# Four 32-column variance tiles a chunk, 128x128 roots between the sigmoids, centring 16 chunks ahead

## The reference, cut to what matters

```
xn    = (x - mean) * rsqrt(var + 1e-5)          # over the 64 channels
left  = (xn @ Wl) * mask * sigmoid(xn @ Wlg)    # layer 3: no mask
right = (xn @ Wr) * mask * sigmoid(xn @ Wrg)
gate  = sigmoid(xn @ Wog)
out   = einsum('bikd,bjkd->bijd', left, right)
out   = layernorm(out) * gate @ Wout
```

## Time and profile before

| | us |
|---|---|
| median of 3 runs (2088.78 to 2090.52) | 2089.22 |
| the profiled execution | 2091.39 |
| its span, which the rows count from | 2089.3 |
| PE busy | 1770.6 (85%) |
| ACT busy | 1372.3 (66%) |
| DVE busy | 1319.1 (63%) |
| POOL busy | 1031.0 (49%) |

### The profile page before, as it was taken

The page is one execution under the profiler, slowest core; times in us unless marked ns, Lnnn a source line. Parts: engine busy times, 40 slices in busy tenths (PEclk is TensorE's granted clock), DMA queues, the critical chain, the costliest instruction groups (busy, mean ns, idle before and its releaser), DMA issues. The chain is left out here.

```text
span 2089.3 us, 41026 instructions
## 1 busy us (share of the span) xinstructions
PE 1770.6 (85%) x10389; PEld 1045.5 (50%) x10389; DVE 1319.1 (63%) x2920; ACT 1372.3 (66%) x2541; POOL 1031.0 (49%) x1044
## 2 busy tenths in 40 slices
PE   0889997797998899985699799799799998699776
PEld 0444454685554444444355477643344444588533
DVE  7566666124763677775977388466377778344675
ACT  0577876365996777774599566477478787244554
POOL 0267678003991677786899200089122223000599
PEclk9999998898999999998899899999899999899999
DMA  7357876774996265647499666189557776845599
GB/s 327 124 184 236 245 232 216 271 297 169 365 367 235 97 189 168 193 135 264 146 357 366 231 226 207 35 321 385 175 157 227 237 236 216 296 174 228 193 398 373
DMA packets 326947, 496.15 MB, mean 237 GB/s; under 512 B 22828, under 2 KB 188463, under 8 KB 320439
## 3 DMA queue, kind: packets, MB, share of 16 engines
q1 hardware_dynamic: 326838, 494.93, 68.4%
HBM read 285.12 MB, written 197.13 MB: 231 GB/s over the span
## 5 line engine op out<-in xcount | busy, mean ns | idle before, releaser
L809 POOL TENSOR_TENSOR lo<-xn,hi 128x512 f16<-128x512 f32 x192 | 224.1, 1167 | 373.5 <-DVE hi L736 231.9
L601 PE MATMUL ps<-w_heads,hi 64*128 64x256 f16 x3072 | 292.8, 273 | 11.7 <-POOL lo L809 4.7
L1118 ACT ACTIVATE O<-ps 128x512 f32 (+1 forms) x144 | 151.7, 1054 | 189.3 <-PE ps L1042 189.3
L750 DVE SCALAR_TENSOR_TENSOR sig<-ps,largest,sig 128x512 f32<-128x512 f32 x256 | 180.7, 746 | 145.4 <-ACT sig L664 144.5
L664 ACT ACTIVATE sig<-ps,largest 128x512 f32<-128x512 f32 x384 | 246.1, 692 | 32.2 <-PE ps L601 23.3
L1355 POOL TENSOR_TENSOR shared<-O,out_rs 128x128 f32<-128x128 f32 (+1 forms) x112 | 76.3, 683 | 371.0 <-DVE out_rs L1255 370.0
L645 ACT ACTIVATE zs<-ps,shift 128x512 f32<-128x512 f32 x192 | 132.0, 687 | 192.9 <-PE ps L569 188.9
L601 PEld LDWEIGHTS ps<-w_heads,hi 64*128 64x128 f16 x3072 | 153.2, 95 | 169.3 <-DVE sig L750 67.0
L1403 PEld LDWEIGHTS ps<-ident,shared 128*128 128x128 f32 (+1 forms) x1024 | 120.2, 133 | 224.8 <-issue 96.8
L1403 PE MATMUL ps<-ident,shared 128*128 128x128 f32 (+1 forms) x1024 | 160.8, 282 | 76.6 <-POOL shared L1355 49.2
L601 PE MATMUL ps<-w_heads,lo 64*128 64x256 f16 x1536 | 212.8, 272 | 0.0
(11 more groups left out here) (168 smaller groups left out, 3787.6 us busy)
## 6 DMA issues: line engine op xcount, KB each, us to landing
shared<-left_right SPq DMA_DIRECT2D x34, 2048.0 KB, 12.0
shared<-gate SPq DMA_DIRECT2D x224, 256.0 KB, 4.6
gate<-gates SPq DMA_DIRECT2D x96, 512.0 KB, 2.9
x_dram<-shared SPq DMA_DIRECT2D x192, 256.0 KB, 4.3
shared<-x_dram SPq DMA_DIRECT2D x192, 256.0 KB, 4.7
xs<-x_dram SPq DMA_DIRECT2D x64, 512.0 KB, 4.2
left_right<-stage SPq DMA_DIRECT2D x64, 448.0 KB, 5.9
left_right<-shared SPq DMA_DIRECT2D x64, 448.0 KB, 5.9
```

What stands on the lines that cost most here:

```text
L601: last = pe.matmul(PAIR[row][:, g, kb * S:kb * S + S], tokens[half, q % 8, at:at + P], k["w_heads"][half, part, :], start=(step == 0), sto ...
L750: dve.scalar_tensor_tensor(dst, pair(row, 1), k["largest"][:, 1:2], factor, ALU.mult, ALU.mult).then_inc(pair_read.sem, 1)
L809: pool.tensor_tensor(lo[:, q % 8, :], xn[:, q % 2, :], hi[:, q % 8, :], ALU.subtract).then_inc(c["lo_done"].sem, 1)
L1118: act.activation(o_of(ch), ps[h % 4 // 2][:, h % 2, :].rearrange("p (b g i) -> p b g i", b=2, g=2), ACT.Copy).then_inc(c["o_copied"].sem, 1)
```

## The change

- VAR becomes 128x128: the 512 positions are cut in four, and each quarter has its own 32 columns of the array and its own 32 partitions of the bank. Variance is four f32 matmuls (8 instructions) of 128 positions each, in place of one (2 instructions) of 512.
- Ln, Exp and the split work on 128x128 in place of 16x512. The split writes `terms`; SP then moves its rows to `r_terms` with 12 DMAs of 16x128 a batch (4 for the first term, 8 for the two others a step later), and spread waits for them.
- Leads: CENTER 16, VARIANCE 15, LOAD 20. Variance stands ahead of the heads in PE's step.
- The rings of `hi` and `lo` go from 8 to 4, and SP's loop is written out.

```diff
-    LOAD, CENTER, VARIANCE, SPLIT, NORM = 14, 12, 11, 3, 2
+    LOAD, CENTER, VARIANCE, SPLIT, MOVE, NORM = 20, 16, 15, (7, 6), (6, 5), 2
+    R_PARTS, MOVES = 2, 3 * CH // P
...
-        Z, VAR, R, GATE = ps[0][:, 0, :], ps[0][:, 1, :], ps[1][:, 0, :], ps[1][:, 1, :]
+        Z, VAR, R, GATE = ps[0][:, 0, :], ps[0][:, 1, 0:P], ps[1][:, 0, :], ps[1][:, 1, :]
...
+            def move_high(i, b):
+                batch = i * (BODY // BATCH) + b
+                sp.wait_ge(c["r_high"].sem, c["r_high"](batch + 1))
+                sp.wait_ge(c["spread_done"].sem, c["spread_done"](batch * BATCH - BATCH))
+                move(0, b)
+            def move_low(i, b):
+                sp.wait_ge(c["r_split"].sem, c["r_split"](i * (BODY // BATCH) + b + 1))
+                move(1, b)
+                move(2, b)
+            def move(term, b):
+                for quad in range(CH // P):
+                    sp.dma_start(r_terms[R_PART * term:R_PART * term + 2 * BATCH, b % 2, quad * P:quad * P + P],
+                                 terms[quad * QUAD:quad * QUAD + 2 * BATCH, term, :]).then_inc(c[f"r_moved{b % 2}"].sem, 16)
             def step(i, q, more, first=False):
+                for part, lead in zip((move_high, move_low), MOVE):
+                    if more(lead) and (q + lead) % BATCH == 0:
+                        part(i, (q + lead) // BATCH)
                 if q % 2 == 0 and more(LOAD):
                     load(i, q + LOAD)
...
-                w = k["var_w"][:, 2 * (BATCH - 1 - at):2 * (BATCH - 1 - at) + P]
-                pe.matmul(VAR, w, sq[:, q % 2, :], start=(at == 0), stop=(at == BATCH - 1)).then_inc(c["var_done"].sem, 1)
+                first = 2 * (BATCH - 1 - at)
+                for quad in range(CH // P):
+                    last = pe.matmul(VAR[quad * QUAD:quad * QUAD + QUAD, :], k["var_w"][:, first:first + QUAD],
+                                     sq[:, q % 2, quad * P:quad * P + P], start=(at == 0), stop=(at == BATCH - 1))
+                last.then_inc(c["var_done"].sem, 1)
...
             def spread(i, q):
-                pe.wait_ge(c["r_split"].sem, c["r_split"](i * (BODY // BATCH) + b + 1))
+                moved = c[f"r_moved{b % 2}"]
+                pe.wait_ge(moved.sem, moved((i * (BODY // BATCH // 2) + b // 2 + 1) * MOVES * 16))
...
                 if more(CENTER):
                     center(i, q + CENTER, Z, i * BODY + q + CENTER)
+                if more(VARIANCE):
+                    variance(i, q + VARIANCE)
                 heads(i, q, 0)
                 heads(i, q, 1)
                 out_gate(i, q)
-                if more(VARIANCE):
-                    variance(i, q + VARIANCE)
...
-                act.activation(log_var[:], VAR[0:2 * BATCH, :], ACT.Ln, bias=k["unit"][0:2 * BATCH, 2:3]).then_inc(c["log_done"].sem, 1)
+                act.activation(log_var[:], VAR, ACT.Ln, bias=k["unit"][:, 2:3]).then_inc(c["log_done"].sem, 1)
...
-                dve.tensor_copy(terms[0], r[:]).then_inc(parts.sem, 1)
...
-                dve.tensor_tensor(terms[2], r_rest[:], r_mid[:], ALU.subtract).then_inc(split.sem, 1)
+                dve.tensor_copy(terms[:, 0, :], r[:]).then_inc(c["r_high"].sem, 1)
...
+                dve.tensor_tensor(r_rest[:], r[:], terms[:, 0, :], ALU.subtract).then_inc(parts.sem, 1)
...
+            def split_low(i, b):
...
+                dve.tensor_copy(terms[:, 1, :], r_rest[:]).then_inc(parts.sem, 1)
...
+                dve.tensor_tensor(terms[:, 2, :], r_rest[:], terms[:, 1, :], ALU.subtract).then_inc(c["r_split"].sem, 1)
```

More of the change, by code:

```diff
@@ L459, in project @@
         xs, zs, sq = sb("xs", [P, 8, CH]), sb("zs", [P, 16, CH]), sb("sq", [P, 2, CH])
[L460 to L461 removed]
+        log_var, r, r_rest = sb("log_var", [P, P]), sb("r", [P, P]), sb("r_rest", [P, P])
+        terms = sb("terms", [P, 3, P], BF16)
         r_terms = sb("r_terms", [P, 2, CH], BF16)
[L463 removed]
+        xn, hi, lo = sb("xn", [P, 2, CH]), sb("hi", [P, 4, CH], F16), sb("lo", [P, 4, CH], F16)
         sig, gates = sb("sig", [P, 4, CH]), sb("gates", [P, 4, CH])
@@ L543, in _ @@
                 load(0, q)
+            move_high(0, 0)
+            move_low(0, 0)
             for q in range(BODY):
                 step(0, q, lambda lead: True, first=True)
-            with sp.Fori(1, bodies - 1) as i:
+            for i in range(1, bodies):
                 for q in range(BODY):
-                    step(i, q, lambda lead: True)
-            for q in range(BODY):
-                step(bodies - 1, q, lambda lead: q + lead < BODY)
+                    step(i, q, lambda lead: i * BODY + q + lead < NCH)
             sp.wait_ge(c["lr_done"].sem, c["lr_done"](NCH * 2))
@@ L600, in heads @@
                             half = slice(g * C, g * C + C)
-                            last = pe.matmul(PAIR[row][:, g, kb * S:kb * S + S], tokens[half, q % 8, at:at + P],
+                            last = pe.matmul(PAIR[row][:, g, kb * S:kb * S + S], tokens[half, q % 4, at:at + P],
                                              k["w_heads"][half, part, :], start=(step == 0), stop=(step == 2))
@@ L665, in gate_pair @@
                                ACT.Sigmoid, scale=k["largest"][:, 0:1]).then_inc(c["sig_done"].sem, 1)
-            def root_step(i, q, more):
-                if more(VARIANCE) and (q + VARIANCE) % BATCH == BATCH - 1:
-                    root(i, (q + VARIANCE) // BATCH)
             def step(i, q, more):
@@ L676, in step @@
                 gate_pair(i, q, 1)
-                root_step(i, q, more)
+                if more(VARIANCE) and (q + VARIANCE) % BATCH == BATCH - 1:
+                    root(i, (q + VARIANCE) // BATCH)
                 act.wait_ge(c["gate_mm_done"].sem, c["gate_mm_done"](m + 1))
@@ L688, in _ @@
                     root(0, 0)
-            start = (2 * BATCH - 1 - VARIANCE) % BATCH + 1
-            for q in range(start):
-                step(0, q, lambda lead: True)
+            step(0, 0, lambda lead: True)
             with act.Fori(0, bodies - 2) as i:
-                for q in range(start, start + BODY):
+                for q in range(1, 1 + BODY):
                     step(i, q, lambda lead: True)
-            for q in range(start, 2 * BODY):
+            for q in range(1, 2 * BODY):
                 step(bodies - 2, q, lambda lead: q + lead < 2 * BODY)
@@ L755, in step @@
                     norm(i, q + NORM)
-                if more(SPLIT) and (q + SPLIT) % BATCH == 0:
-                    split_r(i, (q + SPLIT) // BATCH)
+                for split, lead in zip((split_high, split_low), SPLIT):
+                    if more(lead) and (q + lead) % BATCH == 0:
+                        split(i, (q + lead) // BATCH)
                 left_and_right(i, q)
@@ L831, in project @@
     batches = NCH // BATCH
-    for name in ("log_done", "r_done", "r_split"):
+    for name in ("log_done", "r_done", "r_high", "r_split"):
         c[name].advance(batches)
-    c["r_part"].advance(3 * batches)
+    c["r_part"].advance(R_PARTS * batches)
+    for s in range(2):
+        c[f"r_moved{s}"].advance(16 * MOVES * batches // 2)
     for name in ("z_done", "sq_done", "var_done", "spread_done", "xn_done", "hi_done", "lo_done", "gate_mm_done", "gate_done"):
```

54 lines of the change are left out of this document (26 added, 28 removed).

## The result

The changed kernel takes 2037.79 us (median of 4 runs, 2034.19 to 2040.94), the kernel before beside it 2089.0 (2086.0 to 2090.52). The ratio is 0.9756, 95% interval 0.9733 to 0.9779. The profiled execution took 2034.19 us, with a span of 2032.4.

The account below looks back on a forecast made before the run. PE's instructions were taken to bound the kernel, 4.10 us a step. Gains of 54.6 in the loop and 11.6 in the last steps, less 18.3 ahead of the loops, made 48 us: 2041 for the median, range 1988 to 2092.

Parts of the forecast that it names:

- What bounds the kernel: In the loop PE's instructions follow without a wait, so a chunk costs their sum, 4.10 us, except at the root.
- The variance: PE's variance on column tiles that partly overlap: 5 slots of 0.107, 0.54 us; step 3.88, 0.22 less.
- the first rival: All four column tiles at once: variance 0.22, step 3.56, 50 us less, 1991; chance 0.13.
- The change of shape: A change of tile shape costs PE about 0.10 us, and a step has one such change more.
- The root: Ln and Exp on ACT, with shorter activations: PE loses 1.3 us a batch in place of 2.2.
- SP: SP's queue: 12 moves at about 0.4 us each, 4.8 a batch; 0.3 us a batch added in layers 0 and 3.
- slower rival: Spread waits more than 4 us a batch for the terms in SP's queue; at 6 it is 2113; chance 0.09.
- The starts: Ahead of each layer's loop: 6.1 us more, including 2.5 of waiting for the first terms; 18.3 over three layers.
- The sum: 54.6 us from the loop's batches plus 11.6 from steps without center and variance, less 18.3 ahead of loops: net 48.
- The third rival: Moved terms come 1 to 4 us late in the 12 batches of layers 0 and 3: 2050 to 2085; chance 0.12.
- The second: Rival: no two column tiles at once, variance 0.88, step 4.22, 47 us more, 2088; chance 0.16.
- fourth: The slower rival: spread waits more than 4 us a batch for the terms; chance 0.09.

Follow-up runs that it names:

- e1: Changed kernel, but from a layer's second batch on variance is one f32 matmul on one column tile (three quarters of roots stale): 2095.58 us, 1.0035 to the kernel before.
- e3: Changed kernel with variance back behind the gate's matmuls in PE's step, leads unchanged: 2048.99 us, 0.9823 to the kernel before.
- e10: Changed kernel with first moves ahead of loads 16 and 18, large stores over seven steps, eight gate slots: 2007.32 us, 0.9617 to the kernel before.
- e11: e10 plus the split behind the products on DVE in layer 3 alone: 2002.83 us, 0.9594 to the kernel before.
- e9: Kernel before with the change's leads, variance ahead of the heads, SP's loop written out, and the split 6 steps ahead: 2139.77 us, 1.0247 to the kernel before.
- e5: Changed kernel with a segment's eight large stores issued over seven steps in place of four: 2022.46 us, 0.9688 to the kernel before.
- e4: Changed kernel with the first batch's 12 moves issued ahead of loads 16 and 18: 2022.55 us, 0.9684 to the kernel before.

## Why the prediction came out right, step by step

The forecast of 2041 is 3 us off, and no single part of it was that good. That column tiles which overlap would shorten PE's step, and the kernel with it, was right. The sizes were not, their errors cancelled, and that they did so this closely is luck. By the profiled executions it is 9 us: 2043 was forecast and 2034.2 came, since the one before lies 2.2 above its median and the one after 3.6 below.

- **What bounds the kernel** held. PE's starts still follow one another in the middle of a batch, and a change of PE's step (e1) moved the time by 58 us.
- **The variance: the term that was mis-sized.** "The second pass of a tile must wait for its first, but may run beside the first pass of the next tile. That gives 5 slots of 0.107, or 0.54 us." Measured: two slots of 0.13, not five of 0.107; 0.36 with the change of shape, and at the forecast's own 0.10 for it 0.26, close to the bound of 0.22 which stood for all tiles at once. The four tiles start together, so the assumption that a tile's second pass keeps back the tiles behind it was wrong. The step is 3.60, not 3.88. Over 8 steps and 18 batches of the loop that alone is 40 us more gain; it was the size of the first rival. The heads, from which I took the pattern, alternate between two row tiles only and could show no more than two at once.
- **The change of shape** costs 0.12 in e1 (0.98 less two passes of 0.43) and 0.11 in e3 (3.71 less 3.60) where 0.10 was read from the earlier trace rows. The Trainium skill (TensorEngine Tiling (Array Packing), Key Properties) says that a change of mode drains the engine; here a change costs 0.11 to 0.12 us, and a step has one more than before. Keeping variance next to center paid: e3 is slower.
- **The root.** 1.3 us lost a batch was forecast; 1.8 came in layer 1, and 2.3 and 3.0 in layers 0 and 3 of e10. The 1.8 are all ACT's: 0.72 for the Ln and 0.50 for the gate's sigmoid (0.6 and 0.3 were forecast), and center in the step after, behind the late square. With a shorter step PE arrives sooner at what ACT does no faster, as the first rival said; Ln and Exp themselves took 0.37 and 0.31 where 0.42 and 0.37 were taken. The other 0.5 of layer 0 are the third step, and so the split on DVE; in layer 3 it takes 0.7 (e11). That "the split on 128 columns only shortens DVE's work, which waits for ACT anyway" was wrong there. The split moved away from the root's stop, and its lower half, beside POOL's `lo`, now delays products (in e9 the whole of it does).
- **SP.** 0.4 us a move was taken from one small load; ahead of the loops moves in a row take 0.63 to 0.72, and among the large stores up to 0.95 in layer 0. The terms came late in only a few batches, since they are needed late enough, but what stands behind them in the queue came late too: the gate's stores, which the prediction mentions only in its slower rival. Together the burst cost 15 us (e5); 0.3 us a batch, 3.6 in all, had been set aside.
- **The starts.** From the first center to the first matmul of the gate the three layers take 43.3, 48.0 and 44.4 us, before 33.9, 36.5 and 37.3: 27.9 more, forecast 18.3. The waits for the first terms were 5.3 us each, not 2.5: again the moves, and then a spell at the lower clock.
- **The sum.** From the first to the last matmul of the gate the three layers gained 79.3 us, forecast 66.2 (54.6 and 11.6). Less the starts that is 51.4, and outside these stretches 5.6 more came off, for which the forecast had nothing; together they are the 56.9 by which the spans differ. Forecast was 48. So the 40 us more from the variance were nearly eaten up: the six batches of each layer gained 70 where 54.6 was forecast, since the root, the split and SP took some 25 us more than had been set aside for them.
- **Small slips in the sums.** The three waits of PE for the root add up to 1.2 and not 1.3, and ACT's batch to 26.6 and not 26.8. The third rival, at its own 1 to 4 us in 12 batches, is 2053 to 2089. None of it changes the forecast by more than 2 us.

The rivals: the first was right in mechanism. Its time was not reached even with most of the costs of SP and the starts taken away: e11 stands at 2003 where it said 1991. The second is refuted by the two groups of passes on the trace; e1 is the kernel it describes, and takes 2096 where it said 2088. The third and fourth needed spreads that are late in each batch: in layer 0's loop PE waited 4.8 us in all for moved terms.

## What to carry to other kernels

Here four column tiles of a 128-row f32 matmul worked at once, so a matmul that needs only a few output rows (here 16, in 32 columns of the array) is worth trying with its streamed columns cut into tiles. Other numbers of tiles were not measured. When work is moved away from a stop that everything already waits for, price it anew on its engine: it loses its cover (e9). And many small DMAs in one queue are paid by what stands behind them: issue them ahead of transfers that have no hurry (e4), and do not bunch large stores around them (e5).

## What the runs showed of the hardware

- **Four column tiles of f32.** Eight passes of 128 columns take two slots of 0.13 us, 0.26 in all, where one tile takes 0.86 (e1). The Trainium skill (TensorEngine Tiling (Array Packing), Theoretical Speedup) gives up to four times for a dimension of 32 or less; here it is 0.86 / 0.26, or 3.3, for matmuls of two passes.
- **DVE beside POOL.** A 128x128 subtraction takes 0.29 us alone, and 1.12 when it starts 0.19 after POOL's `lo`. In both cases shown it ends 0.15 to 0.16 after POOL does (170.92 after 170.76, 177.01 after 176.86). The trace has 42 of them in the loops. All start beside an operation of POOL, take 0.59 to 1.28 us, and end 0.15 after it. The 16x512 subtraction of e9 takes 1.52, and 0.68 in the kernel before, where POOL is idle. It is a wait, not a slower rate. The Trainium skill (SBUF — State Buffer, SBUF: two separate sides) states an exclusive lock between GpSimd and a DVE operation with two SBUF inputs; the trace agrees.
- **Small DMAs.** 4 KB moves take SP 0.63 us each in a row (7.59 for 12) and 0.86 among the large stores of the batch shown (6.88 for 8), while a single load took 0.36.
- **The clock.** After 5 us with 0.08 us of work PE was at 0.50 for 7 us, and its matmuls took 1.5 to 1.9 times as long (0.66 for 0.43, 1.92 for 1.02).
